# Prologue and first tile of a four-layer token kernel merged into one order of steps, the exact matmul form placed directly behind its branches, and the last block's statistics moved

## What is computed

```python
x = x + L0_attn(layernorm(x))   # linear attention: phi(q) @ (phi(k).T @ v), phi = silu + 1, 16 heads
x = x + L0_ffn(layernorm(x))    # silu(x W1) * (x W2) -> gelu(H1) -> gelu(H2) -> W3, hidden size 1024,
                                # weights are -1, 0 or 1, with a scale for each output
x = x + L1_attn(layernorm(x))   # softmax attention, one head of 256
x = x + L1_ffn(layernorm(x))    # tanh(x Wa Wb Wc + bias), the three weights folded into one
```

## Time and profile before

| | |
|---|---|
| median of 3 runs | 2023.21 us (2021.99 to 2027.07) |
| the profiled execution | 2024.01 us, its span in the trace 2022.3 us |
| TensorE | busy 1987.7 us, 98% of the span |
| VectorE | busy 1178.3 us, 58% |
| ScalarE | busy 826.2 us, 41% |
| GpSimd | busy 373.5 us, 18% |
| granted TensorE clock, mean | 0.994 of full |

### The profile page before, as it was taken

How to read it: one execution, slowest core, us unless ns; L and a number is a source line. 1 busy time by engine, 2 the same in 40 slices (tenths; PEclk the granted TensorE clock), 3 DMA queues, 4 the chain that set the end, 5 groups by cost and what they waited for, 6 DMA issues and landing times.

```text
span 2022.3 us, 37442 instructions
## 1 busy us (share of the span) xinstructions
PE 1987.7 (98%) x15512; PEld 1922.6 (95%) x15512; DVE 1178.3 (58%) x2886; ACT 826.2 (41%) x1532; POOL 373.5 (18%) x350
## 2 busy tenths in 40 slices
PE   7999999999999999999999999999999999999996
PEld 6899999999999999999999999999999999999996
DVE  5645657466574655656456574665656556564456
ACT  2334434344344444434444343444444444344333
POOL 2011211112121121210212121121211212111111
PEclk9999999999999999999999999999999999999999
DMA  9500000000000000000000000000000000000000
GB/s 345 227 3 2 22 1 1 22 1 22 1 22 1 1 22 1 22 1 1 22 1 22 1 12 12 1 22 1 22 1 1 22 1 12 1 1 11 1 1 22
DMA packets 24533, 46.01 MB, mean 23 GB/s; under 512 B 1264, under 2 KB 21488, under 8 KB 24176
## 3 DMA queue, kind: packets, MB, share of 16 engines
q1 hardware_dynamic: 24352, 43.41, 6.0%
HBM read 35.02 MB, written 19.92 MB: 27 GB/s over the span
## 4 chain that ended last, share of the span: by engine, by line
PE 95%; DMA 2%; DVE 1%; issue 1%; SPq 0%; ACT 0%; POOL 0%; POOLq 0%; DVEq 0%; ACTq 0%
PE ffn_fill L1049 48%; PE att_fill L999 25%; PE ffn_fill L999 12%; PE ffn_fill L1107 6%; PE att_fill L1067 2%; PE att_fill L1184 1%; DMA scratch_h1T<-in_h1T 1%; PE ffn_fill L1075 1%; DMA h<-scratch_h1T 1%; DMA scratch_w2T<-in_w2T 1%; SPq L541 0%; DVE lowsum L892 0%; DVE prob_t_lo L828 0%; DVE late_sm L833 0%; POOL rstd_E L637 0%
## 5 line engine op out<-in xcount | busy, mean ns | idle before, releaser
L1049 PE MATMUL ffn_fill<-act_hi,h 128*128 128x256 f32 x4096 | 987.1, 283 | 0.4
L1049 PE MATMUL ffn_fill<-act_lo,h 128*128 128x256 f32 x4096 | 978.4, 281 | 0.0
L1049 PEld LDWEIGHTS ffn_fill<-act_hi,h 128*128 128x128 f32 x4096 | 770.9, 188 | 6.7 <-POOL act_lo L651 3.8
L1049 PEld LDWEIGHTS ffn_fill<-act_lo,h 128*128 128x128 f32 x4096 | 772.7, 189 | 3.0
L931 ACT ACTIVATE whole<-ffn_fill,scales 128x256 f32<-128x256 f32 x512 | 214.5, 470 | 396.3 <-PE ffn_fill L1049 338.3
L766 DVE CAST act_hi<-whole 128x512 fp32r<-128x512 f32 x256 | 108.2, 423 | 311.5 <-ACT whole L931 311.5
L651 POOL TENSOR_TENSOR act_lo<-whole,act_hi 128x512 fp32r<-128x512 f32 x128 | 167.9, 1311 | 497.5 <-DVE act_hi L762 497.5
L999 PE MATMUL ffn_fill<-half_hi,w 128*128 128x256 f32 x1024 | 249.3, 284 | 4.7 <-issue 2.4
L999 PE MATMUL ffn_fill<-half_lo,w 128*128 128x256 f32 x1024 | 246.7, 282 | 0.0
L999 PEld LDWEIGHTS ffn_fill<-half_hi,w 128*128 128x128 f32 x1024 | 193.7, 189 | 5.0 <-issue 4.9
L999 PEld LDWEIGHTS ffn_fill<-half_lo,w 128*128 128x128 f32 x1024 | 194.3, 190 | 0.0
(11 more groups left out here) (232 smaller groups left out, 3179.3 us busy)
## 6 DMA issues: line engine op xcount, KB each, us to landing
x<-in_L_attn_x SPq DMA_DIRECT2D x16, 512.0 KB, 3.7
out<-x SPq DMA_DIRECT2D x15, 512.0 KB, 3.0
h<-scratch_h1T SPq DMA_DIRECT2D x2, 2048.0 KB, 15.0
h<-scratch_h2T SPq DMA_DIRECT2D x2, 2048.0 KB, 14.9
w<-scratch_w1T SPq DMA_DIRECT2D x1, 1024.0 KB, 5.4
w<-scratch_w2T SPq DMA_DIRECT2D x1, 1024.0 KB, 7.5
w<-scratch_w3T SPq DMA_DIRECT2D x1, 1024.0 KB, 7.7
rows<-in_rows SPq DMA_DIRECT2D x1, 640.0 KB, 6.0
```

The source lines that it names most:

```text
L1049: last = pe.matmul(two(bank)[:, o, :], view(w), view(moving[:, k, :]), start=k == 0 and o == 0 and half == 0, stop=k == KH - 1 and half == ...
```

## The change

- `PROLOGUE` and `FIRST` become one list and one order for each engine. Tile 1's first attention (`a:`) starts in what was the prologue, ahead of `U0`, and its `AS` and `AQ` stand between `U0` and `U2`, ahead of `CHECK1`; before, they stood behind `CHECK1`. `f:FA0` moves behind `p:AM`, `f:FA1` and `f:FA2` behind `a:T`, and `WARM4` goes.
- On ScalarE `LOOK00` moves ahead of `p:AQ`.
- `SQUARED` goes from 768 to 1024: of each 2048 elements ScalarE takes 1024, VectorE 1024 instead of 1280.
- `ANO` on VectorE gets a wait for the query parts of the attention before, whose buffer it overwrites; they are made by VectorE itself, further up in its own order.
- Both branches are turned round, so that the exact form stands directly behind the compare and the float32 form behind it.
- In `END`, `d:ES3` moves ahead of `d:ET2` and `d:EF2`, `d:EN2` behind `c:CF`, `c:DST` ahead of `d:ES0`, `c:T` ahead of `d:CP2` on TensorE, and a few more steps change places by one.

```diff
-SQUARED = 768
+SQUARED = 1024
...
-PROLOGUE = steps_from("""
-    WARM24 a:AST a:ANO a:AB PREP0 a:T a:AKV0 SCALE a:AKV1 a:AKV2 a:AKV3 PREP1 a:AS f:FA0 a:AQ f:FA1 a:AM f:FA2 LOOK00 LOOK01
-    f:TA0 a:AO f:TA1 n:BST0 f:TA2 n:BNO0 WARM4 n:BT0 CHECK0""")
 FIRST = steps_from("""
...
 PE_ORDERS = {
-    "PROLOGUE": order_from("""
-    WARM24 a:T a:AKV0 a:AKV1 a:AKV2 a:AKV3 f:FA0 a:AS a:AQ a:AM a:AO f:FA1 f:FA2 WARM4 n:BT0 CHECK0"""),
     "FIRST": order_from("""
-    U0 U1 U2a a:T U2b U3a a:AKV0 a:AKV1 a:AKV2 a:AKV3 U3b CHECK1 a:AS a:AQ G0a a:AM G0b G1a a:AO G1b G2a
...
+    WARM24 p:T p:AKV0 p:AKV1 p:AKV2 p:AKV3 p:AS p:AQ p:AM f:FA0 p:AO a:T f:FA1 f:FA2 a:AKV0 CHECK0 a:AKV1
+    a:AKV2 m:BT0 a:AKV3 U0 a:AS U1a a:AQa U1b a:AQb U2 U3 CHECK1 a:AM G0a a:AO G0b G1 G2 FOLD0 G3a CHECK2
...
 ACT_ORDERS = {
-    PREP0 a:T a:AKV0 a:AKV1 a:AKV2 a:AKV3 PREP1 a:AQ a:AM LOOK00 LOOK01 n:BT0"""),
+    PREP0 p:T p:AKV0 p:AKV1 p:AKV2 p:AKV3 PREP1 LOOK00 p:AQ p:AM LOOK01 a:T a:AKV0 a:AKV1 m:BT0 a:AKV2
...
                 elif kind in ("ANO", "CNO", "DNO"):
+                    if kind == "ANO":
+                        wait(dve, s["phiq_ready"], c.value("phiq_ready"))
                     normalise(c, own, x[:, slots[who]], own.xn, "A" if kind == "ANO" else "E" if who == "d" else "C", NB)
...
-                with pe.If(flags[layer] != 0):
-                    emit(lambda ap: ap.bitcast(F32))
-                with pe.Else():
-                    emit(lambda ap: ap)
+                with pe.If(flags[layer] == 0):
+                    emit(lambda ap: ap)
+                with pe.Else():
+                    emit(lambda ap: ap.bitcast(F32))
...
-            with pe.If(inexact != 0):
+            with pe.If(inexact == 0):
+                plain["form"] = lambda ap: ap
+                walk_rest(part, PE_ORDERS)
+            with pe.Else():
                 plain["form"] = lambda ap: ap.bitcast(F32)
                 walk_rest_looped(pe, part, PE_ORDERS)
-            with pe.Else():
-                plain["form"] = lambda ap: ap
-                walk_rest(part, PE_ORDERS)
```

More of the change, by code:

```diff
@@ L219, in before @@
     return None if isinstance(value, int) and value <= 1 else value - 1
-PROLOGUE = steps_from("""
-    WARM24 a:AST a:ANO a:AB PREP0 a:T a:AKV0 SCALE a:AKV1 a:AKV2 a:AKV3 PREP1 a:AS f:FA0 a:AQ f:FA1 a:AM f:FA2 LOOK00 LOOK01
-    f:TA0 a:AO f:TA1 n:BST0 f:TA2 n:BNO0 WARM4 n:BT0 CHECK0""")
 FIRST = steps_from("""
-    U0 a:AST U1 a:ANO U2 a:T U3 LOOK10 a:AB a:AKV0 a:AKV1 LOOK11 a:AKV2 LOOK12 a:AKV3 LOOK13 CHECK1 a:AS a:AQ
+    WARM24 p:AST p:ANO p:AB PREP0 p:T p:AKV0 SCALE p:AKV1 p:AKV2 p:AKV3 PREP1 p:AS f:FA0 p:AQ a:AST f:FA1 p:AM f:FA2
+    f:TA0 p:AO a:ANO a:T LOOK00 LOOK01 f:TA1 m:BST0 a:AKV0 a:AKV1 f:TA2 m:BNO0 m:BT0 CHECK0
+    U0 U1 U2 U3 LOOK10 a:AB LOOK11 a:AKV2 LOOK12 a:AKV3 LOOK13 CHECK1 a:AS a:AQ
     G0 a:AM G1 a:AO WIDE G2 LOOK20 LOOK21 FOLD0 TAKE0 G3 LOOK22 LOOK23 CHECK2 LOOK30
@@ L233 @@
     d:CS0 d:CS1 c:CP2 c:CO2 c:CP3 c:CO3 d:CP0 d:CO0 c:DST d:CS2 d:CP1 d:ES0 d:CO1 d:EN0 c:DNO d:CS3 d:ET0 c:T d:ES1 d:EN1
-    d:CP2 d:EF0 c:CF d:CO2 d:ET1 d:EF1 d:ES2 d:CP3 d:EN2 d:CO3 d:ET2 d:EF2 d:ES3 d:EN3 d:ET3 d:EF3""")
+    d:CP2 d:EF0 c:CF d:CO2 d:ET1 d:EF1 d:ES2 d:CP3 d:EN2 d:CO3 d:ES3 d:ET2 d:EF2 d:EN3 d:ET3 d:EF3""")
 def order_from(plan):
@@ L258 @@
 DVE_ORDERS = {
-    "PROLOGUE": order_from("""
-    a:AST a:ANO PREP0 a:T a:AKV0 SCALE a:AKV1 a:AKV2 a:AKV3 PREP1 a:AS f:TA0 a:AQ a:AM LOOK00 LOOK01 a:AO
-    n:BST0 f:TA1 n:BNO0 f:TA2 CHECK0 n:BT0"""),
     "FIRST": order_from("""
-    a:AST U0 a:ANO LOOK10 a:T U1 LOOK11 a:AKV0 a:AKV1 a:AKV2 a:AKV3 LOOK12 LOOK13 U2 CHECK1 a:AS U3 a:AQ
-    a:AM LOOK20 a:AO LOOK21 WIDE LOOK22 LOOK23 LOOK30 G0 TAKE0 CHECK2 G1 G2 CHECK3 G3 H0 BST1 H1 H2 BNO1 H3
-    BT1 W0 n:BST0 U0 U1 U2 U3 G0 G1 G2 n:BNO0 G3 H0 H1 H2 H3 n:BT0 W1"""),
+    p:AST p:ANO PREP0 p:T p:AKV0 SCALE p:AKV1 p:AKV2 p:AKV3 PREP1 p:AS a:AST p:AQ p:AM LOOK00 LOOK01 a:ANO
+    p:AO m:BST0 a:T f:TA0 CHECK0 a:AKV0 f:TA1 m:BNO0 a:AKV1 m:BT0 a:AKV2 a:AKV3 f:TA2 U0 LOOK10 a:AS LOOK11
+    U1 a:AQ LOOK12 LOOK13 CHECK1 U2 a:AM U3 a:AO G0 LOOK20 WIDE LOOK21 LOOK22 LOOK23 G1 LOOK30 TAKE0 G2
+    CHECK2 G3 CHECK3 BST1 H0 BNO1 n:BST0 H1 H2 H3 BT1 W0 U0 U1 U2 U3 G0 G1 G2 n:BNO0 G3 H0 H1 H2 H3 n:BT0 W1"""),
     "BODY": order_from("""
@@ L270 @@
     "END": order_from("""
-    U0 U1 U2 U3 G0 G1 G2 G3 H0 H1 BST1 BNO1 H2 H3 BT1 W0 U0 U1 U2 U3 G0 c:CST G1 G2 G3 H0 c:CNO H1 H2 c:T
+    U0 U1 U2 U3 G0 G1 G2 G3 H0 H1 BST1 H2 BNO1 H3 BT1 W0 U0 U1 U2 U3 G0 G1 G2 c:CST G3 H0 c:CNO H1 H2 c:T
     c:CQ H3 W1 d:CST c:CV d:CNO c:CZ d:LT c:CS0 c:CS1 d:CQ c:CP0 c:CO0 c:CP1 d:CV d:CZ c:CO1 c:CS2 d:CS0
-    c:CS3 d:CS1 c:CP2 d:CP0 c:CO2 c:CP3 d:CO0 d:CS2 c:CO3 d:CP1 d:ES0 c:DST d:CO1 d:EN0 d:CS3 c:DNO d:ET0
-    d:ES1 d:EN1 d:CP2 d:EF0 c:T d:CO2 d:ET1 d:EF1 d:ES2 d:CP3 d:EN2 c:CF d:CO3 d:ET2 d:EF2 d:ES3 d:EN3 d:ET3
+    c:CS3 d:CS1 c:CP2 d:CP0 c:CO2 c:CP3 d:CO0 d:CS2 c:CO3 d:CP1 c:DST d:ES0 d:CO1 d:EN0 d:CS3 c:DNO d:ET0
+    d:ES1 d:EN1 d:CP2 d:EF0 c:T d:CO2 d:ET1 d:EF1 d:ES2 d:CP3 c:CF d:EN2 d:CO3 d:ES3 d:ET2 d:EN3 d:EF2 d:ET3
     d:EF3"""),
@@ L291 @@
 POOL_ORDERS = {
[L292 to L293 removed]
     "FIRST": order_from("""
[L295 removed]
+    p:AST a:AST p:AB m:BST0 U0 U1 a:AB U2 U3 BST1 n:BST0 U0 U1 U2 U3"""),
     "BODY": order_from("""
@@ L298 @@
     "END": order_from("""
-    U0 U1 U2 U3 BST1 U0 U1 U2 U3 c:CST d:CST d:CB c:CB d:ES0 c:DST d:ES1 d:EF0 d:EF1 d:ES2 c:CF d:EF2 d:ES3
+    U0 U1 U2 U3 BST1 U0 U1 U2 U3 c:CST d:CST d:CB c:CB d:ES0 c:DST d:ES1 d:EF0 d:EF1 d:ES2 c:CF d:ES3 d:EF2
     d:EF3"""),
@@ L421, in build @@
         phases = []
[L422 to L425, removed]
+        phases.append(dict(start))
+        for n, k in total(FIRST).items():
+            start[n] = start.get(n, 0) + k
         phases.append(dict(start))
@@ L577, in _ @@
             c = Counts(phases[0])
-            for step in PROLOGUE + FIRST:
+            for step in FIRST:
                 if step[:2] == ("FOLD", 0):
```

26 lines of the change are left out of this document (12 added, 14 removed).

## The result

The changed kernel takes 2018.12 us (median of 8 runs, 2015.67 to 2020.37); the kernel before, on the same chip, 2023.03 (8 runs). The ratio is 0.9971 with a 95% interval of 0.996 to 0.9982: it is faster, by some 5 us, where 12.5 were predicted, and 2018.12 lies above the range that was given.

The account below looks back on a forecast made before the run. TensorE, 95% of the chain that ended last, was taken to bound the kernel. First tile 6.2, branches 4.1 and end 2.2 sum to 12.5 us (0.6%), giving a median of 2010.7 us; range 2007.8 to 2015.5.

Parts of the forecast that it names:

- The gap at `BODY`: At 156.42 us, TensorE's 2.40 us stall from the far jump and 1.7 us of half speed go: 4.1 us.
- Rival 2: Far jump's stall stays wherever the load and new code stand: 8.4 us gained, 2014.8; with rival 3 together 0.17.
- The far jump at TensorE's end: The jump moves to TensorE's end, where other engines and the store have some 4 us left, hiding 2.4.
- The 30 inner branches at 0: First tile: branches swap a jump ahead of their matmuls for one behind; no gap shows, so 0 us.
- rival 4: First tile's 30 products each end in a taken jump that may cost; at 0.9 us each 2037.7; chance 0.03.
- The end, 2.2 us: Last block's chain: normalise 1.8 us sooner, up to 0.7 more behind it; 2.2 taken, bounds 0 and 2.9.
- The first tile, 6.2 us: `CHECK1` 0.5 us sooner, 6.3 us of `AS` and `AQ` gone behind it, less 0.6 for an uncovered flag load.
- The wait for H1 covers all of these: First tile: H1's landing at 58.5 us hides TensorE's later work, ready at 58.5 to 59.5, or 61.
- The first is covered: Half speed behind the 2.5 to 3.3 us wait before `p:AO` costs nothing.
- rival 1: The clock: half speed behind `CHECK1`'s gap costs 1.7 us, leaving 10.8 us gained, 2012.4; chance 0.27.
- rival 3: Prologue late beyond its cover, VectorE being busy: with 4 us lost 8.5 remain, 2014.7; with Rival 2 together 0.17.
- Behind `CHECK1`: First tile: only `AM` stands between `CHECK1` near 61.1 and `G0` near 62.5 us, instead of 68.13.

Follow-up runs that it names:

- before_end: The kernel before with only the changed kernel's orders of `END`, on all engines: 2020.88 us, ratio 0.9988.
- before_turned: The kernel before with only its last branch turned round, exact side first: 2021.87 us, ratio 0.9994.
- before_inner_turned: The kernel before with only the 30 branches of the first tile's products turned round: 2025.58 us, ratio 1.001.
- after_look_back: The changed kernel with `LOOK00` on ScalarE put back behind `p:AM`: 2013.24 us, ratio 0.9951 to the kernel before.
- after_kept_busy: The changed kernel with 24 extra transposes of the identity on TensorE in its wait ahead of `p:AO`: 2014.63 us, ratio 0.9958 to the kernel before.
- after_squared_768: The changed kernel with `SQUARED` put back from 1024 to 768: 2017.33 us, ratio 0.9972 to the kernel before.
- after_bias_early: The changed kernel with GpSimd's `a:AB` (tile 1's bias sum) moved directly behind `p:AB`: 2015.39 us, ratio 0.9957 to the kernel before.
- after_one_side: The changed kernel without the float32 side of the last branch: 2016.61 us, ratio 0.9969 to the kernel before.

## Why the prediction was wrong, by its steps

- **The gap at `BODY`: right.** 2.40 us and the half-speed stretch are gone, 3.9 in all for 4.1. Rival 2 (the stall stays) is out. That the half speed always comes with the gap isn't so: before_end had 2.29 us of gap and none behind it.
- **The far jump at TensorE's end: the step that failed in the branch's term.** "VectorE, ScalarE, GpSimd and the store ... have some 4 us to go, which hide 2.4." They hide TensorE's standing, but the second page that the jump fetches is read while the last store is under way, and the store lands 2.2 us later in the trace. In before_turned that takes back 2.0 of the 4.1 us.
- **The 30 inner branches at 0: right** for the first tile (92.36 against 92.42 us); rival 4 is out. That before_inner_turned is 2 us slower was not foreseen, and one near jump in one trace did stall, by 1.9 us.
- **The end, 2.2 us: right within its bounds, in part by luck.** The normalise comes 2.1 us sooner behind the attention output, where 1.8 were expected; from there to the last sum nothing was gained (4.88 us against 4.86), where up to 0.7 were. It makes 1.9 us in the changed kernel's trace, 1.5 in that of before_end, and 2.2 by the medians of before_end.
- **The first tile, 6.2 us: wrong**, 0.07 in the profiled run. The failed sentence is "The wait for H1 covers all of these". I followed TensorE alone: it was at `CHECK1` at 60.88, within what was said (58.5 to 61). But `CHECK1` needs VectorE's looks, and VectorE was at `a:AQ` till 62.2, so the looks came 3.9 us behind H1. Three things made it late. The first is `LOOK00`'s wait for W1: after_look_back takes it away, the half speed behind it goes too, and the looks start as H1 lands. The second is that half speed behind `p:AO`, which "The first is covered" (rival 1) held to be harmless: after_kept_busy, with the wait and without the half speed, gains 2.6 to 3.5 of the 4.0 to 4.9 us of after_look_back. In its trace and in that of after_squared_768 the looks start 2.3 and 2.1 us behind H1 at full clock, so the wait and the third thing make them late even without the clock. The third is that `a:AQ` was stretched by 3.0 us beside GpSimd's `U1` and `a:AB`; after_bias_early takes away the 2.0 beside `a:AB`, and for the 1.0 beside `U1` there is no run. That is rival 3, with 3.5 us lost at `CHECK1` (64.60 against 61.1).
- **Behind `CHECK1`:** 1.4 us to `G0` were predicted, 2.42 came, and half speed ran on to 70.9: rival 1, and with two stretches instead of one. From `CHECK1` to `BODY` it took 89.35 us, where the sum of the prediction gives 86.7 (154.0 less 6.2, less 61.1). So rivals 1 and 3 came together, at 2.6 and 3.5 us; I had priced each alone. With the store's 2.2, 0.2 at the branch (3.9 for 4.1) and 0.3 at the end (1.9 for 2.2) they are the 8.8 us between 12.5 and 3.7.
- The 0.07 us of the first tile are the difference of two single runs. `W1` ends between 154.02 and 155.27 in the four traces with before's first tile as it stands, and `BODY` begins at 153.95 and 154.97 in the two traces with the changed one as it stands (the second is after_one_side). By the medians the first tile did somewhat better: 4.9 in all, less 1.2 (before_turned) and 2.2 (before_end), leaves some 1.5 us.

The Trainium skill's page "SBUF — State Buffer" (section "SBUF: two separate sides") says that a VectorE operation with two SBUF inputs and a GpSimd operation that reads SBUF exclude each other: whichever starts first has the shared ports for its whole instruction, and the other waits. The rows agree nearly: `qz_lo` starts at 57.51, GpSimd's `act_lo` ends at 58.63, and 0.69 behind that would be 59.32; it ended at 59.18. The rows also show `qz_hi`, with one input, held up: it took 1.52 us beside `a:AB` instead of 0.42. Read for this change, the rule would have made `a:AB` beside `a:AQ` a term of the sum.

## What to carry to other kernels

Work that is moved ahead of a wait on a transfer is free only if every engine in the chain behind that transfer is ready for it; follow each of them, with the durations that its operations have beside their new neighbours. A wait of TensorE may cost more in clock behind it, and differently from run to run: put useful work into it before trying to shorten it. Here `FOLD0` was put there, together with `a:AB` early, for 3.2 us over after_look_back by the medians and 3.8 by the ratios. And compare a change of a few us in several traces: here two traces of the same first tile differed by 1.25 us. A far jump moved to an engine's end still fetches code, and the last store may be under way beside that fetch.
